# A four-layer sequence kernel on one core: router, tile sum and attention in 32-column tiles, one input share for all gates, one activation over candidate and i

## The chip, the cores and the metric

One program runs on one core of a Trainium2 chip. The metric is the device time of one execution in microseconds (us), from a handful of runs; the profiled execution gives a trace of every instruction beside its own time. A smaller time is better.

## What is computed

The input x is 2 sequences (B = 2) of 1024 tokens with 256 features, with one conditioning vector per sequence. Four layers are added to x one after the other:

```
x = x + attention(x, cond)       # 16 heads, two keys per token: a fixed one and one from cond
x = x + experts(x, cond)         # shared SwiGLU unit + top 2 of 8 GELU experts, a router picks them
x = x + (gelu(cond@W_proj+b)@W_u + x@W_e)
x = x + lstm(x, h0=cond)         # below
```

The last layer is a recurrence over the 1024 tokens and cannot be made parallel in time:

```
xz = x@Wx + b                                # (2, 1024, 4*256)
z = xz_t + prev_h @ Wh
ai, af, ao, ag = split(z, 4)                 # i, f, o and the candidate c (ag)
next_c = sigmoid(af) * prev_c + sigmoid(ai) * tanh(ag)
next_h = sigmoid(ao) * tanh(next_c)
```

All sigmoids are written as tanh of half the argument, so that one table of ScalarE serves.

## The kernel before

**Batches and steps.** The tokens are worked in 128 batches of U = 8 steps. A step is one token of both sequences. Each engine has its own program with its own loop over the batches; inside it the eight steps u = 0 to 7 are written out. Nothing but semaphores orders the engines against one another. The engines are TensorE (PE), VectorE (DVE), ScalarE (ACT), GpSimd (POOL) and SyncE (SP), which only moves x in and y out.

**The chain of one step.** PE multiplies the last h (`h_ring`) with Wh. For the gates f and i the small h is the stationary operand and the weights move (`recur_row`, 64 columns wide); the result lies in rows and DVE has to transpose it (`t_f`, `t_i`). For the candidate c and for o the weights are stationary and h moves (`recur_column`, 2 columns wide); that result needs no transpose. All of them are written in 32-column tiles: four matmuls (j = 0 to 3) that use the four column groups of the array. Each fp32 matmul of the program is two matmul instructions in the trace. Then ACT takes tanh of f, of c and of i; DVE makes `keep_out` (f times the old cell) and, by a scan, the new cell; ACT takes tanh of o and of the cell; DVE makes h, which increments `hid`, and PE's next step waits for `hid`.

**Side work.** Everything else is done for later batches between the steps: after its recurrence matmuls PE does, in u = 0, `stream_mm` and `down_mm(0)`; in u = 1 `scores` and `route`; in u = 2 `down_mm(1)` and `down_mm(2)`; in u = 3 `sum_mm` and `attend`; in u = 4 and 5 `up_mm`; in u = 6 and 7 the input share x@Wx of the next eight steps.

**The input share.** z_f, z_i, z_c and z_o hold the eight steps of a batch in PSUM. Before the change DVE copies the bias into them (`bias_f`, `bias_i`, `bias_x`) and PE adds x@Wx: `inject_x` (c and o, 128 columns wide, u = 6) and two calls of `inject` (f, i, 64 wide, u = 7). c and o come out in rows in `z_x`, and DVE transposes them at the head of the loop, in u = 0, into z_c and z_o (L689, L690); PE's first c matmul of the batch waits for that (`x_turned`).

**Names of lines.** L921 is `recur_row`, L931 `recur_column`, L709 and L711 the transposes of f and i, L507, L510, L513, L516, L519 the tanh of f, c, i, o and cell, L717 `keep_out`, L720 the scan, L738 h, L604, L607, L610 the bias copies, L767 `scores`, L777 and L779 `route`, L807 `sum_mm`, L771 `attend`, L784 `up_mm`, L790 `stream_mm` and `down_mm`, L825 and L818 the input share.

## Time and profile before

| | |
|---|---|
| time, median of 3 runs | 2076.67 us (2074.86 to 2077.8) |
| profiled execution | 2075.86 us, of which 2074.1 us are the span of the trace |
| PE matmul busy | 2023.7 us, 98% |
| PE weight loads busy | 1620.8 us, 78% |
| DVE busy | 1368.1 us, 66% |
| ACT busy | 910.0 us, 44% |
| POOL busy | 1139.5 us, 55% |
| DMA | 7 GB/s on average |

Busy is the time in which at least one instruction of the engine was under way, as a share of the span. Matmuls are pipelined and overlap one another, so 98% doesn't mean that the array has no room. The span is nearly all loop: the recurrence begins some 45 us into it and runs 128 batches.

### The profile page before, as it was taken

Reading aid. Unit: us, or ns where it says so; the run is one execution under the profiler, and the core shown is the slowest. Engines: PE = TensorE matmul, PEld = TensorE weight load, DVE = VectorE, ACT = ScalarE, POOL = GpSimd, SP = SyncE. Lnnn points to the kernel's source line nnn. Section 1 sums busy time; section 2 is a strip of 40 time slices with the busy share of each in tenths; the row PEclk is TensorE's granted clock in tenths of the full one; section 3 lists DMA queues with packets and bytes.
Section 4 is the critical chain, followed back from the end, with each engine's and each line's share of the span. In section 5 each row is a group of like instructions: output and inputs, shape, how many; then the busy total and the mean of one; then the engine's idle time right before and its main releaser. Section 6 shows DMA issues by size and latency. Waiting matters only on the chain. (4 is left out here: it accounts for less than half of the span.)

```text
span 2074.1 us, 254185 instructions
## 1 busy us (share of the span) xinstructions
PE 2023.7 (98%) x112624; PEld 1620.8 (78%) x112624; DVE 1368.1 (66%) x7216; ACT 910.0 (44%) x5781; POOL 1139.5 (55%) x4950
## 2 busy tenths in 40 slices
PE   7999999999999999999999999999999999999999
PEld 6777777777777777777777777777777777777777
DVE  2566666666666666666666666666666666666666
ACT  1344444444444444444444444444444444444444
POOL 3555555555555555555555555555555555555555
PEclk9999999999999999999999999999999999999999
DMA  4000000000000000000000000000000000000000
GB/s 160 4 3 3 3 4 3 3 3 3 3 3 4 3 3 3 3 3 3 3 3 3 3 3 3 3 3 3 3 4 3 3 3 3 3 3 4 3 3 3
DMA packets 57724, 14.67 MB, mean 7 GB/s; under 512 B 56176, under 2 KB 56304, under 8 KB 57200
## 3 DMA queue, kind: packets, MB, share of 16 engines
q1 hardware_dynamic: 57712, 14.50, 3.0%
q8 instruction: 9, 0.15, 0.0%
q14 instruction: 3, 0.02, 0.0%
HBM read 12.37 MB, written 2.10 MB: 7 GB/s over the span
## 5 line engine op out<-in xcount | busy, mean ns | idle before, releaser
L931 PE MATMUL bank<-h_ring,wh_sb 128*32 128x2 f32 x65536 | 765.6, 173 | 1.8 <-issue 1.8
L921 PEld LDWEIGHTS bank<-wh_sb,h_ring 128*2 128x2 f32 (+1 forms) x32768 | 480.0, 90 | 331.1 <-DVE h_ring L738 320.8
L931 PEld LDWEIGHTS bank<-h_ring,wh_sb 128*32 128x32 f32 x65536 | 731.0, 109 | 2.0 <-issue 2.0
L921 PE MATMUL bank<-wh_sb,h_ring 128*2 128x64 f32 (+1 forms) x32768 | 658.3, 220 | 18.0 <-issue 2.5
L507 ACT ACTIVATE f_act<-bank 128x4 f32<-128x4 f32 x1024 | 177.3, 173 | 781.3 <-DVE bank L709 772.7
L709 DVE STREAM_TRANSPOSE bank<-bank 128x64 f32<-128x64 f32 x1024 | 270.3, 264 | 312.3 <-PE bank L921 296.7
L784 PE MATMUL bank<-up_sb,x 128*32 128x512 f32 x2064 | 283.2, 606 | 0.0
L711 DVE STREAM_TRANSPOSE bank<-bank 128x64 f32<-128x64 f32 x1024 | 270.8, 264 | 0.6 <-PE bank L921 0.6
L790 PE MATMUL bank<-down_e,hid_t 128*16 128x256 f32 x3096 | 268.5, 381 | 0.6 <-ACT down_e L488 0.6
L720 DVE TENSOR_TENSOR_SCAN bank<-addend,bank 128x16 f32<-128x16 f32 x1024 | 200.3, 196 | 103.4 <-ACT bank L513 2.7
L738 DVE SCALAR_TENSOR_TENSOR h_ring<-o_act,bank 128x4 f32<-128x4 f32 x1024 | 159.9, 156 | 119.0 <-ACT bank L519 87.0
L380 POOL TENSOR_TENSOR num<-one,fall 128x8 f32<-128x8 f32 x128 | 25.6, 200 | 353.5 <-ACT fall L467 353.5
L516 ACT ACTIVATE o_act<-bank 128x4 f32<-128x4 f32 x1024 | 177.3, 173 | 70.3 <-PE bank L931 1.4
L717 DVE SCALAR_TENSOR_TENSOR addend<-f_act,bank 128x4 f32<-128x4 f32 x1024 | 165.9, 162 | 21.4
L510 ACT ACTIVATE bank<-bank 128x4 f32<-128x4 f32 x1024 | 161.8, 158 | 41.4 <-PE bank L931 2.7
L519 ACT ACTIVATE bank<-bank 128x4 f32<-128x4 f32 x1024 | 161.8, 158 | 21.4
L513 ACT ACTIVATE bank<-bank 128x4 f32<-128x4 f32 x1024 | 158.7, 155 | 0.0
L790 PEld LDWEIGHTS bank<-down_e,hid_t 128*16 128x16 f32 x3096 | 102.4, 95 | 41.3 <-issue 1.5
L386 POOL TENSOR_TENSOR num<-num 128x8 f32<-128x8 f32 x520 | 103.6, 199 | 40.8
L818 PE MATMUL bank<-wx_sb,x 128*16 128x64 f32 x4128 | 107.4, 222 | 8.7
L825 PE MATMUL bank<-wx_sb,x 128*16 128x128 f32 x2064 | 81.3, 275 | 10.0 <-issue 0.4
L432 POOL TENSOR_TENSOR hid_e<-gelu_act,gate_w 128x256 f32<-128x256 f32 x130 | 79.7, 613 | 17.2
(144 smaller groups left out, 2543.9 us busy)
## 6 DMA issues: line engine op xcount, KB each, us to landing
x_a<-in_x SPq DMA_DIRECT2D x129, 16.0 KB, 1.7
x_s<-in_x SPq DMA_DIRECT2D x129, 16.0 KB, 1.6
up_sb<-in_up SPq DMA_DIRECT2D x1, 2048.0 KB, 12.6
out_y<-y_sb SPq DMA_DIRECT2D x128, 16.0 KB, 1.4
down_sb<-in_down SPq DMA_DIRECT2D x1, 1536.0 KB, 8.1
wx_sb<-in_wx SPq DMA_DIRECT2D x1, 1024.0 KB, 14.8
wh_sb<-in_wh SPq DMA_DIRECT2D x1, 1024.0 KB, 16.8
wkv_sb<-in_wkv SPq DMA_DIRECT2D x1, 512.0 KB, 3.8
```

What stands on the lines that cost most here:

```text
L507: nc.scalar.activation(f_act[:, :].rearrange("p (c b) -> p c b", b=B), by_row(t_f)[:, :, step], ACT.Tanh).then_inc(a_f, 1)
L510: nc.scalar.activation(factor_q[:, :, 2].rearrange("p (c b) -> p c b", b=B), by_row(z_c)[:, :, step], ACT.Tanh)
L516: nc.scalar.activation(o_act[:, :].rearrange("p (c b) -> p c b", b=B), by_row(z_o)[:, :, step], ACT.Tanh)
L519: nc.scalar.activation(c_tanh, cell_c, ACT.Tanh).then_inc(cell_tanh, 1)
L709: nc.vector.transpose(t_f, z_f).then_inc(f_turned, 1)
L711: nc.vector.transpose(t_i, z_i).then_inc(i_turned, 1)
L717: nc.vector.scalar_tensor_tensor(out=keep_out, in0=f_act[:, :], scalar=1.0, in1=cell_c, op0=ALU.add, op1=ALU.mult).then_inc(terms_in, 1)
L720: nc.vector.tensor_tensor_scan(cell_all, addend[:, :], factor, 0.0, ALU.add, ALU.mult).then_inc(cell, 1)
L784: last = nc.tensor.matmul(units[32 * j:32 * (j + 1), :], src[:, c, 0, :], up_sb[:, c, j, :], start=(c == 0), stop=(c == C - 1), skip_group ...
L790: return nc.tensor.matmul(partial_b[32 * j:32 * j + NB, :], lhs, rhs, start=first, stop=False, skip_group_check=True)
L921: last = nc.tensor.matmul(z[32 * j:32 * j + row + B, :], h_ring[:, prev, c, WIN - B - row:WIN], wh_v[:, c, g, j, :], start=False, stop=(c ...
L931: last = nc.tensor.matmul(by_row(z)[32 * j:32 * (j + 1), m, row:row + B], wh_v[:, c, g, j, 32 * m:32 * (m + 1)], h_ring[:, prev, c, WIN - ...
```

## The change

1. `route`, `sum_mm` and `attend` no longer use 128-column stationary operands. Each matmul is split into four of 32 columns (j = 0 to 3), each to its own quarter of the partitions. The matmul with `pick` in `route` (L779 before) stays at 128 columns.
2. The input share of all four gates is made by one `inject` in u = 6, 256 columns wide, into a wider `z_x`; the wait for `terms_in` ahead of it is gone, and so are both injects in u = 7. DVE writes all four biases with one copy in u = 5 (`bias_x`, 256 wide in place of 128), and no longer in u = 7.
3. z_f gets its share by a copy from z_x in u = 7 (`base_f`, where `bias_f` was, with one more wait, for `x_injected`); z_i by a copy at the head of the loop in u = 0, ahead of the two transposes. PE waits for `f_based` and `i_based` in u = 0.
4. One activation makes tanh of c and of i together (8 elements a partition instead of twice 4). It waits for the count `i_and_c_in`, which DVE's transpose of i and PE's c matmuls both raise. For it t_i and z_c are placed in neighbouring banks; z_o gets a bank of its own.
5. In the part ahead of the loop the folded weights rotate through five banks instead of four, and some small results lie in other banks.

```diff
@@ -179,21 +179,28 @@
         addend = sb("addend", [P, 4 * NCELL])
         keep_out = addend[:, :].rearrange("p (q k) -> p q k", k=4)[:, :, 3]
 
-        bank = [ctx.enter_context(nc.psum_tensor(f"bank{n}", [P, 512], F32)) for n in range(8)]
-
-
-
-        z_f, z_i = bank[0][:, 0:HC], bank[1][:, 0:HC]
+        BANK = 512
+        psum = ctx.enter_context(nc.psum_tensor("psum", [P, 8 * BANK], F32))
+        bank = [psum[:, n * BANK:(n + 1) * BANK] for n in range(8)]
+
+
+
+        z_f, z_i = bank[0][:, 0:HC], bank[3][:, 0:HC]
         t_f = bank[6][:, 4 * HC:5 * HC]
-        t_i = bank[1][:, HC:2 * HC]
-        z_x = bank[2][:, HC:3 * HC]
-        z_c, z_o = bank[2][:, 0:HC], bank[3][:, 0:HC]
+        z_x = bank[2][:, 0:4 * HC].rearrange("p (g m) -> p g m", g=4)
+        z_o = bank[1][:, 0:HC]
+
+        T_I, Z_C = 3 * BANK + HC, 4 * BANK
+        t_i, z_c = psum[:, T_I:T_I + HC], psum[:, Z_C:Z_C + HC]
+        i_and_c = psum[:, T_I:T_I + 2 * (Z_C - T_I)].rearrange("p (g k) -> p g k", g=2)[:, :, 0:HC]
+        i_and_c = i_and_c.rearrange("p g (c r) -> p g c r", r=32)
...
         factor = bank[4][:, HC:HC + 4 * NCELL]
         factor_q = factor.rearrange("p (q k) -> p q k", k=4)
+        i_and_c_out = factor_q[:, :, 1:3].rearrange("p q g -> p g q")
...
-                    act.wait_ge(c_made, now)
-                    nc.scalar.activation(factor_q[:, :, 2].rearrange("p (c b) -> p c b", b=B),
-                                         by_row(z_c)[:, :, step], ACT.Tanh)
-                    act.wait_ge(i_turned, now)
-                    nc.scalar.activation(factor_q[:, :, 1].rearrange("p (c b) -> p c b", b=B),
-                                         by_row(t_i)[:, :, step], ACT.Tanh).then_inc(terms_in, 1)
+                    act.wait_ge(i_and_c_in, act.snap(t * 2 + (2 * u + 2)))
+                    nc.scalar.activation(i_and_c_out.rearrange("p g (c b) -> p g c b", b=B),
+                                         i_and_c[:, :, :, step], ACT.Tanh).then_inc(terms_in, 1)
...
-
-            def bias_f(up_to):
-                nc.vector.tensor_copy(z_f, bias_sb[:, GF, :]).then_inc(f_bias, up_to)
-
-            def bias_i(up_to):
-                nc.vector.tensor_copy(z_i, bias_sb[:, GI, :]).then_inc(i_bias, up_to)
-
             def bias_x(up_to):
-                nc.vector.tensor_copy(z_x.rearrange("p (g m) -> p g m", g=2),
-                                      bias_sb[:, GO:GC + 1, :]).then_inc(x_bias, up_to)
+
+                nc.vector.tensor_copy(z_x, bias_sb[:, :, :]).then_inc(x_bias, up_to)
+
+
+            def base_f(up_to):
+                nc.vector.tensor_copy(z_f, z_x[:, GF, :]).then_inc(f_based, up_to)
 
...
             with dve.Fori(READY, READY + T, U) as t:
@@ -685,9 +687,9 @@
                     now = dve.snap(t + (u + 1))
                     if u == 0:
 
-                        dve.wait_ge(x_injected, now)
-                        nc.vector.transpose(z_c, z_x[:, HC:2 * HC])
-                        nc.vector.transpose(z_o, z_x[:, 0:HC]).then_inc(x_turned, U)
+                        nc.vector.tensor_copy(z_i, z_x[:, GI, :]).then_inc(i_based, U)
+                        nc.vector.transpose(z_c, z_x[:, GC, :])
+                        nc.vector.transpose(z_o, z_x[:, GO, :]).then_inc(x_turned, U)
                     elif u == 1:
                         dve.wait_ge(x_ready, now)
                         dve.wait_ge(stream_made, now)
@@ -708,10 +710,11 @@
                     dve.wait_ge(f_made, now)
                     nc.vector.transpose(t_f, z_f).then_inc(f_turned, 1)
                     dve.wait_ge(i_made, now)
-                    nc.vector.transpose(t_i, z_i).then_inc(i_turned, 1)
+                    nc.vector.transpose(t_i, z_i).then_inc(i_and_c_in, 1)
                     if u == 7:
                         dve.wait_ge(f_turned, now)
-                        bias_f(U)
+                        dve.wait_ge(x_injected, now)
+                        base_f(U)
 
                     dve.wait_ge(a_f, now)
                     nc.vector.scalar_tensor_tensor(out=keep_out, in0=f_act[:, :], scalar=1.0, in1=cell_c,
@@ -728,7 +731,6 @@
                     elif u == 6:
...
-                        bias_i(U)
...
             def attend(attn, weights):
                 for c in range(C):
-                    last = nc.tensor.matmul(attn[:, c], value_w[:, c * P:(c + 1) * P], weights,
-                                            start=True, stop=True)
+                    for j in range(J):
+                        last = nc.tensor.matmul(attn[32 * j:32 * (j + 1), c],
+                                                value_w[:, c * P + 32 * j:c * P + 32 * (j + 1)], weights,
+                                                start=True, stop=True, skip_group_check=True)
                 return last
 
             def route(out, src):
                 for c in range(C):
-                    nc.tensor.matmul(out, src[:, c, :, :].rearrange("p j n -> p (j n)"), router[:, c, :],
-                                     start=(c == 0), stop=False, skip_group_check=True)
+                    for j in range(J):
+                        nc.tensor.matmul(out[32 * j:32 * (j + 1), :], src[:, c, j, :], router[:, c, :],
+                                         start=(c == 0), stop=False, skip_group_check=True)
                 nc.tensor.matmul(out, pick, route_t[:, :], start=False, stop=True,
                                  skip_group_check=True).then_inc(route_made, U)
 
@@ -804,27 +809,21 @@
 
             def sum_mm():
                 for c in range(C):
-                    last = nc.tensor.matmul(x3_b[:, c, :], partial[:, c * P:(c + 1) * P], sum_tiles,
-                                            start=True, stop=True)
+                    for j in range(J):
+                        last = nc.tensor.matmul(x3_b[32 * j:32 * (j + 1), c, :],
+                                                partial[:, c * P + 32 * j:c * P + 32 * (j + 1)], sum_tiles,
+                                                start=True, stop=True, skip_group_check=True)
                 return last
...
-            def inject(z, g):
+            def inject():
 
                 for c in range(C):
                     for j in range(J):
-                        last = nc.tensor.matmul(z[32 * j:32 * j + NB, :], x3[:, c, NB:2 * NB], wx_v[:, c, g, j, :],
-                                                start=False, stop=False, skip_group_check=True)
-                return last
-
-            def inject_x():
-                for c in range(C):
-                    for j in range(J):
-                        last = nc.tensor.matmul(z_x[32 * j:32 * j + NB, :].rearrange("p (g m) -> p g m", g=2),
-                                                x3[:, c, NB:2 * NB], wx_v[:, c, GO:GC + 1, j, :],
-                                                start=False, stop=False, skip_group_check=True)
+                        last = nc.tensor.matmul(z_x[32 * j:32 * j + NB, :, :], x3[:, c, NB:2 * NB], wx_v[:, c, :, j, :],
+                                                start=False, stop=(c == C - 1), skip_group_check=True)
                 return last
...
                     prev = (u - 1) % U
                     now = pe.snap(t + (u + 1))
                     pe.wait_ge(hid, now)
+                    if u == 0:
+                        pe.wait_ge(f_based, now)
                     recur_row(z_f, GF, u * B, prev).then_inc(f_made, 1)
+                    if u == 0:
+                        pe.wait_ge(i_based, now)
                     recur_row(z_i, GI, u * B, prev).then_inc(i_made, 1)
                     if u == 0:
                         pe.wait_ge(x_turned, now)
-                    recur_column(z_c, GC, u * B, prev).then_inc(c_made, 1)
+                    recur_column(z_c, GC, u * B, prev).then_inc(i_and_c_in, 1)
                     recur_column(z_o, GO, u * B, prev).then_inc(o_made, 1)
...
                     elif u == 6:
-
-                        pe.wait_ge(terms_in, pe.snap(t * 2 + (2 * u + 2)))
                         pe.wait_ge(x_bias, now)
-                        inject_x().then_inc(x_injected, U)
-                    elif u == 7:
-                        pe.wait_ge(f_bias, now)
-                        inject(z_f, GF)
-                        pe.wait_ge(i_bias, now)
-                        inject(z_i, GI)
+                        inject().then_inc(x_injected, U)
```

The first place is DVE's row at the head of the loop, u = 0. Before:

```order
L683 ISA
L689 STREAM_TRANSPOSE bank<-bank 128x64 [waits x_injected]
L690 STREAM_TRANSPOSE bank<-bank 128x64
L709 STREAM_TRANSPOSE bank<-bank 128x64 [waits f_made]
L711 STREAM_TRANSPOSE bank<-bank 128x64 [waits i_made]
```

And of the changed kernel:

```order
L690 COPY psum<-psum 128x64
L691 STREAM_TRANSPOSE psum<-psum 128x64
L692 STREAM_TRANSPOSE psum<-psum 128x64
L710 REGISTER_ALU
L711 STREAM_TRANSPOSE psum<-psum 128x64 [waits f_made]
L713 STREAM_TRANSPOSE psum<-psum 128x64 [waits i_made]
```

The copy of z_i now stands ahead of the two transposes; the wait and the register instruction for it (ISA) are gone from the head.

The second place is PE's row from the c and o matmuls of u = 6 to the end of the loop. Before:

```order
L931 MATMUL bank<-h_ring,wh_sb 32x2 x32
L976 ISA
L825 MATMUL bank<-wx_sb,x 16x128 [waits x_bias,terms_in]
L825 MATMUL bank<-wx_sb,x 16x128 x7
L941 REGISTER_ALU
L921 MATMUL bank<-wh_sb,h_ring 16x64 [waits hid]
L921 MATMUL bank<-wh_sb,h_ring 16x64 x15
L931 MATMUL bank<-h_ring,wh_sb 32x2 x32
L818 MATMUL bank<-wx_sb,x 16x64 [waits f_bias]
L818 MATMUL bank<-wx_sb,x 16x64 x7
L818 MATMUL bank<-wx_sb,x 16x64 [waits i_bias]
L818 MATMUL bank<-wx_sb,x 16x64 x7
```

And of the changed kernel:

```order
L926 MATMUL psum<-h_ring,wh_sb 32x2 x32
L825 MATMUL psum<-wx_sb,x 16x256 [waits x_bias]
L825 MATMUL psum<-wx_sb,x 16x256 x7
L936 REGISTER_ALU
L916 MATMUL psum<-wh_sb,h_ring 16x64 [waits hid]
L916 MATMUL psum<-wh_sb,h_ring 16x64 x15
L926 MATMUL psum<-h_ring,wh_sb 32x2 x32
L932 REGISTER_ALU
L932 COMPARE_AND_BRANCH
```

All of the input share now stands in u = 6, and in u = 7 the loop's branch comes right behind the recurrence matmuls.

The third place is ACT's row in a step. Before:

```order
L507 ACTIVATE f_act<-bank 128x4 [waits f_turned]
L510 ACTIVATE bank<-bank 128x4 [waits c_made]
L513 ACTIVATE bank<-bank 128x4 [waits i_turned]
L516 ACTIVATE o_act<-bank 128x4 [waits o_made]
L519 ACTIVATE bank<-bank 128x4 [waits cell]
```

And of the changed kernel:

```order
L517 ACTIVATE f_act<-psum 128x4 [waits f_turned]
L519 REGISTER_ALU
L520 ACTIVATE psum<-psum 128x2x4 [waits i_and_c_in]
L523 ACTIVATE o_act<-psum 128x4 [waits o_made]
L526 ACTIVATE psum<-psum 128x4 [waits cell]
```

Two activations became one, with a register instruction ahead of it that works out the count to wait for.

## Rows read from the trace of the kernel before

**Rows 1.** Page, busy time of each engine, share of the span, instructions.

```profile
PE 2023.7 (98%) x112624; PEld 1620.8 (78%) x112624; DVE 1368.1 (66%) x7216; ACT 910.0 (44%) x5781; POOL 1139.5 (55%) x4950
```

**Rows 2.** Timeline (start us, us, engine, line, x instructions), PE L921: first matmuls of steps.

```profile
1000.19 0.63 PE L921 MATMUL bank<-wh_sb,h_ring 128*4 128x64 f32 x32
...
1002.22 0.63 PE L921 MATMUL bank<-wh_sb,h_ring 128*6 128x64 f32 x32
...
1004.12 0.64 PE L921 MATMUL bank<-wh_sb,h_ring 128*8 128x64 f32 x32
...
1006.24 0.64 PE L921 MATMUL bank<-wh_sb,h_ring 128*10 128x64 f32 x32
...
1008.14 0.66 PE L921 MATMUL bank<-wh_sb,h_ring 128*12 128x64 f32 x32
...
1010.03 0.66 PE L921 MATMUL bank<-wh_sb,h_ring 128*14 128x64 f32 x32
...
1011.92 0.64 PE L921 MATMUL bank<-wh_sb,h_ring 128*16 128x64 f32 x32
...
1014.08 0.63 PE L921 MATMUL bank<-wh_sb,h_ring 128*2 128x64 f32 x32
...
1015.97 0.63 PE L921 MATMUL bank<-wh_sb,h_ring 128*4 128x64 f32 x32
```

**Rows 3.** Timeline, step u = 5 of the same batch.

```profile
1008.59 0.73 PE L931 MATMUL bank<-h_ring,wh_sb 128*32 128x2 f32 x63
...
1008.84 0.27 DVE L711 STREAM_TRANSPOSE bank<-bank 128x64 f32<-128x64 f32 x1
...
1008.91 0.17 ACT L507 ACTIVATE f_act<-bank 128x4 f32<-128x4 f32 x1 [1.03 <-DVE bank L709]
...
1009.13 0.16 ACT L510 ACTIVATE bank<-bank 128x4 f32<-128x4 f32 x1
1009.15 0.19 PEld L784 LDWEIGHTS bank<-up_sb,x 128*32 128x32 f32 x8
...
1009.20 0.15 ACT L513 ACTIVATE bank<-bank 128x4 f32<-128x4 f32 x1
1009.39 0.20 DVE L720 TENSOR_TENSOR_SCAN bank<-addend,bank 128x16 f32<-128x16 f32 x1
...
1009.49 0.27 DVE L610 COPY bank<-bias_sb 128x128 f32<-128x128 f32 x1
...
1009.81 0.16 DVE L738 SCALAR_TENSOR_TENSOR h_ring<-o_act,bank 128x4 f32<-128x4 f32 x1
```

**Rows 4.** Groups by line and form, ACT, from 80 to 2070 us.

```profile
L467 ACT ACTIVATE fall<-bank 128x8 f32<-128x8 f32 x126 | 22.3, 177 | 71.1 <-PE bank L779 71.1
```

**Rows 5.** Timeline, side work of u = 3.

```profile
1005.25 0.62 PE L807 MATMUL bank<-small_sb,partial 128*128 128x16 f32 x4
```

**Rows 6.** Timeline, side work and h of u = 1.

```profile
1001.25 0.27 PE L767 MATMUL bank<-x_s,score_w 128*32 128x16 f32 x4
...
1001.86 0.16 DVE L738 SCALAR_TENSOR_TENSOR h_ring<-o_act,bank 128x4 f32<-128x4 f32 x1
```

**Rows 7.** Timeline, side work of u = 2.

```profile
1003.25 1.07 PE L790 MATMUL bank<-down_e,hid_t 128*16 128x256 f32 x16
```

**Rows 8.** Timeline, DVE across the end of the loop, u = 7 to u = 0.

```profile
1013.28 0.20 DVE L607 COPY bank<-bias_sb 128x64 f32<-128x64 f32 x1
...
1013.62 0.14 DVE L738 SCALAR_TENSOR_TENSOR h_ring<-o_act,bank 128x4 f32<-128x4 f32 x1
...
1013.97 0.27 DVE L689 STREAM_TRANSPOSE bank<-bank 128x64 f32<-128x64 f32 x1 [0.22 <-issue]
...
1014.15 0.22 DVE L690 STREAM_TRANSPOSE bank<-bank 128x64 f32<-128x64 f32 x1
```

**Rows 9.** Windows: busy of PE, PEld, DVE, ACT, POOL; clock; DMA share; GB/s.

```profile
56.20:63.00 6.80, 6.21 (x203) 3.89 (x196) 2.14 (x12) 1.28 (x10) 4.49 (x19) 0.50 0.03 6
...
1000.00:1008.00 8.00, 8.00 (x431) 6.72 (x426) 5.29 (x28) 3.61 (x23) 3.08 (x13) 1.00 0.04 6
```

More of the change, by code:

```diff
@@ L39 @@
 BLOCKS = UNITS * KS
-FOLD = (0, 1, 2, 3)
+FOLD = (0, 1, 2, 3, 4)
 FOLD_1, FOLD_2 = 3, 7
@@ L209, in cond_stack_kernel @@
         attn_first_b = bank[6][:, 128:128 + 2 * C * NB].rearrange("p (c n t) -> p c n t", c=C, n=2)
+        route_t_b = bank[7][0:B, 448:448 + E]
+        u_b = bank[6][:, 400:400 + C * B].rearrange("p (c b) -> p c b", b=B)
+        cond_b = bank[6][:, 408:408 + C * B].rearrange("p (c b) -> p c b", b=B)
         route_first_b = bank[5][:, 64:64 + 2 * E].rearrange("p (n e) -> p n e", n=2)
@@ L270, in cond_stack_kernel @@
         x3_out = sem("x3_out")
-        z_ready = sem("z_ready")
         moved = sem("moved")
         bias_scaled = sem("bias_scaled")
-        f_bias = sem("f_bias")
-        i_bias = sem("i_bias")
         x_bias = sem("x_bias")
+        f_based = sem("f_based")
+        i_based = sem("i_based")
         x_injected = sem("x_injected")
@@ L281, in cond_stack_kernel @@
         i_made = sem("i_made")
-        c_made = sem("c_made")
         o_made = sem("o_made")
         f_turned = sem("f_turned")
-        i_turned = sem("i_turned")
+        i_and_c_in = sem("i_and_c_in")
         a_f = sem("a_f")
@@ L341, in _ @@
             pool.sem_inc(y_stored, 16)
-            for s in (f_made, i_made, c_made, o_made, f_turned, i_turned, a_f, cell, cell_tanh, hid, x_turned):
+            for s in (f_made, i_made, o_made, f_turned, a_f, cell, cell_tanh, hid, x_turned, i_based):
                 pool.sem_inc(s, READY)
             pool.sem_inc(terms_in, 2 * READY)
+            pool.sem_inc(i_and_c_in, 2 * READY)
             pool.sem_inc(own_out, READY)
@@ L443, in _ @@
             weigh(2 * U).then_inc(hid_e_out, 2 * U)
-            pool.wait_ge(z_ready, 1)
+            pool.wait_ge(x_injected, READY)
             move().then_inc(moved, READY + U)
@@ L627, in _ @@
             dve.wait_ge(value_made, 2)
-            nc.vector.tensor_copy(route_t[0:B, :], bank[4][0:B, 0:E]).then_inc(value_out, 1)
+            nc.vector.tensor_copy(route_t[0:B, :], route_t_b).then_inc(value_out, 1)
             dve.wait_ge(w_in["x_first"], 16)
@@ L639, in _ @@
             dve.wait_ge(u_made, 1)
[L640 to L641 removed]
+            nc.vector.tensor_tensor(u_in[:, :, :], u_b, pairs(b_proj2), ALU.add).then_inc(u_in_out, 1)
             dve.wait_ge(w_in["bias_z"], 16)
@@ L650, in _ @@
             dve.wait_ge(cond_made, 1)
-            nc.vector.tensor_copy(cond_t[:, :, :], bank[4][:, D:D + C * B].rearrange("p (c b) -> p c b", b=B)
-                                  ).then_inc(cond_done, 1)
+            nc.vector.tensor_copy(cond_t[:, :, :], cond_b).then_inc(cond_done, 1)
             dve.wait_ge(hid_e_out, U)
@@ L663, in _ @@
             invert_s(2 * U)
+            hidden_a(2 * U)
+            hidden_s(2 * U)
+            dve.wait_ge(fold_out, BLOCKS)
             dve.wait_ge(terms_set, 1)
@@ L680, in _ @@
             invert_inv(2 * U)
+            dve.wait_ge(x_injected, READY)
+            base_f(READY + U)
             dve.wait_ge(terms_set, 3)
@@ L839, in _ @@
             for c in range(C):
-                last = nc.tensor.matmul(bank[4][0:B, 0:E], cond[:, c, :], router_t[:, c, :],
+                last = nc.tensor.matmul(route_t_b, cond[:, c, :], router_t[:, c, :],
                                         start=(c == 0), stop=(c == C - 1))
@@ L879, in _ @@
                 for c in range(C):
-                    last = nc.tensor.matmul(bank[4][:, 64 + m * B:64 + (m + 1) * B],
+                    last = nc.tensor.matmul(u_b[:, m, :],
                                             wproj2_sb[:, c, m * P:(m + 1) * P],
@@ L893, in _ @@
                 for m in range(C):
-                    last = nc.tensor.matmul(bank[4][:, D + c * B:D + (c + 1) * B], wu_sb[:, m, c * P:(c + 1) * P],
+                    last = nc.tensor.matmul(cond_b[:, c, :], wu_sb[:, m, c * P:(c + 1) * P],
                                             u_act[:, m, :], start=(m == 0), stop=(m == C - 1))
@@ L908, in _ @@
             pe.wait_ge(x_bias, READY)
-            inject_x().then_inc(x_injected, READY + U)
-            pe.wait_ge(f_bias, READY)
-            inject(z_f, GF)
-            pe.wait_ge(i_bias, READY)
-            inject(z_i, GI).then_inc(z_ready, 1)
+            inject().then_inc(x_injected, READY)
             pe.wait_ge(own_first, 2)
@@ L974, in _ @@
                     elif u == 6:
-                        pe.wait_ge(terms_in, pe.snap(t * 2 + (2 * u + 2)))
                         pe.wait_ge(x_bias, now)
-                        inject_x().then_inc(x_injected, U)
-                    elif u == 7:
-                        pe.wait_ge(f_bias, now)
-                        inject(z_f, GF)
-                        pe.wait_ge(i_bias, now)
-                        inject(z_i, GI)
+                        inject().then_inc(x_injected, U)
 _INS = ("x", "small", "wkv", "wq", "wproj", "up", "we", "down", "wproj2", "wu", "wx", "wh", "bias_z")
```

7 lines of the change are left out of this document (removed).

## The prediction

> **What bounds the kernel now.** I read the page first. PE is busy 98% of the span, the others 66% or less [rows 1]. That says only that some matmul is nearly always under way, so I went to the timeline of one batch. The starts of the first matmul of each step [rows 2] give the lengths: u = 1 takes 2.03 us (1000.19 to 1002.22), u = 2 1.90, u = 3 2.12, u = 4 1.90, u = 5 1.89, u = 6 1.89, u = 7 2.16, u = 0 1.89; together 15.78 us. 128 batches make 2020 of the 2074 us span. Three steps stand out: u = 1 by 0.14 us, u = 3 by 0.23, u = 7 by 0.27 over 1.89.
>
> What sets 1.89 is seen in u = 5 [rows 3], which begins at 1008.14 [rows 2]. The c and o matmuls begin 0.45 us later (1008.59). ACT's tanh of c starts at 1009.13, that of i at 1009.20, 0.07 behind it and not earlier, though i was transposed by 1009.11. It ends at 1009.35, the scan starts at 1009.39, h at 1009.81, that is 1.67 after the step's start, ends at 1009.97, and 0.06 later PE begins the next step. This is the h chain.
>
> There is a second limit of nearly the same length, the array itself. In u = 2 the 16 side matmuls of 256 columns begin at 1003.25 [rows 7] and the next step at 1004.12, 0.87 later; in u = 5 the weights of `up_mm` begin to load at 1009.15 [rows 3] and the next step starts at 1010.03, 0.88 later. 0.45 for f and i, 0.56 for c and o (1008.59 to 1009.15) and 0.87 make 1.88 to 1.90: a step with this much side work can't be shorter, however early h is. That holds for u = 2, 4 and 5, and, as an estimate, for u = 0: its 12 matmuls of 256 columns give two of the column groups four each, as in u = 2.
>
> **Tiles in u = 3.** `sum_mm` is four instructions from 1005.25 on [rows 5], `attend` four more, and the next step begins 0.99 after 1005.25: 0.12 for each. The h chain would have allowed 1004.12 + 1.67 + 0.16 + 0.06 = 1006.01; it was 1006.24. Now there are 32 instructions of 32 columns, spread over the four column groups. The nearest row is L931, the same tile form with a 2-column moving operand: 63 in 0.73, less 0.17 for the last, so 0.009 apart [rows 3]. 32 of them take 0.29. They may begin at 1005.13 (two thirds of the 0.12 before were a change of form, my estimate) and are over long before 1006.0. u = 3 falls back to the h chain: 0.23 gained. Cover gone, it would be lost again only if the tiles took over 0.8 us.
>
> **Tiles in u = 1.** h ends at 1002.02 [rows 6] and the next step could start at 1002.08; it starts at 1002.22. The router's four instructions of 128 columns (0.12 each, as in u = 3, 0.47 in all) become 16 of 0.009, 0.15 in all. `pick` stays. The array is free at 1002.22 - 0.32 = 1001.90, before h. Gained: 0.14.
>
> **One activation.** It starts when the later of c and i is ready: c at 1009.13 as L510 did, i at 1009.11 plus some 0.03. It lasts 0.16, as L510; four more elements cost under 0.01 (L467 with 8 columns lasts 177 ns [rows 4], L507 with 4 columns 0.17 [rows 3]). So it ends at 1009.30 instead of 1009.35, and the scan comes 0.05 earlier. `keep_out` is done by then. ACT's new register instruction falls in the 0.22 between L507 and L510. This 0.05 counts only in steps that the h chain sets: all of it in u = 3, some 0.02 in u = 1 (there the transposes come later, behind `attended`), and in u = 7. In u = 0, 2, 4, 5 the array takes it back.
>
> **u = 6.** The inject is now 16 instructions of 256 columns, the form of [rows 7]; it need not wait for `terms_in`. It becomes a step at the array's limit: 1.89 to 1.90 instead of 1.89. Lost: 0.01. The bias copy in u = 5 grows from 128 to 256 columns. 64 columns take 0.20 [rows 8], 128 take 0.27 [rows 3], so 256 some 0.40: from 1009.44 to 1009.84. h may start up to 0.05 late by it, which the array's limit hides.
>
> **The loop's end.** PE starts u = 0 at 1014.08, 0.32 after h ended (1013.62 + 0.14 [rows 8]) instead of 0.06: its last inject and its branch lie there. Both are out of the way now. But DVE has a chain of its own: its first instruction of the batch starts 0.35 after h starts (1013.97), the second 0.18 later, ends at 1014.37, and PE needs it for c at 1014.08 + 0.45 = 1014.53. Now h starts at 1.67 - 0.05 = 1.62 of the step, at 1013.54 (the copy of bias i that stood between is gone). Behind it come the copy of z_i, the two transposes, and 0.05 or 0.06 to PE. Slow ends: 1013.54 + 0.35 + 0.18 + 0.18 + 0.22 + 0.06 = 1014.53, nothing gained. Fast ends: the order shows the register instruction gone from the head, so 0.28 instead of 0.35 (an estimate), and a 0.20 long operation lets the next start 0.10 later (L720 to L610 [rows 3]): 1014.38, 0.15 gained. z_i reaches PE in time in both: copied by 1014.15 at the latest, its matmuls done 0.22 later. I take 0.09, nearer to the fast end because of the shorter copy. It is passed on whole: after c, u = 0 runs at the array's limit.
>
> **The sum.** u = 3 0.23 + 0.05, u = 1 0.14 + 0.02, loop's end 0.09, u = 6 -0.01: 0.52 us a batch, 66.6 us in 128. Ahead of the loop 48 narrow injects become 16 wide ones and some matmuls are tiled; some tenths to 2 us, I take 2. The profiled execution took 2075.86, so 2007 us. The median of the runs is 0.8 above it, within their spread of 3 us.
>
> **Rival 1: the small tiles are not side by side.** `scores` has four instructions of 32 columns in one column group, 0.27 less 0.17, so 0.03 apart [rows 6]. If 8 or 16 moving columns cost that much on all groups, u = 3 has 32 x 0.03 = 0.96 of side work, from 1005.13 to 1006.09 and a next step at 1006.15: 0.09 gained. u = 1 has 0.48, as before: nothing. With 0.09 at the loop's end and -0.01: 0.17, 22 us, 2054 us. For it: the narrow form is not shown with these operands. Against: L931 is narrower still and runs at 0.009. The Trainium skill has a rule in this direction (TensorEngine Tiling (Array Packing), Performance Considerations, Instruction Overhead): each matmul has about 60 cycles of overhead, and one should not tile a dimension where the moving side is already small. By it, at 25 ns each, the 32 instructions would take 0.80, the 16 router ones 0.40, the sum 0.38 a batch and the time some 2027 us; L931's rows go against its use here.
>
> **Rival 2: only the tiles gain.** The activation of both waits for the slower of two and its wider form costs what it saves; the loop's end goes by its slow values. Then 0.23 + 0.14 - 0.01 = 0.36, 46 us, 2030 us.
>
> **Rival 3, slower: the clock.** From 56.2 to 63.0 us the granted clock was 0.50 (the 1.2 GHz level), and 203 matmuls were done in 6.8 us; at 1.00 it was 431 in 8.0, which is 366 in 6.8 [rows 9]. Such a stretch loses 3.0 us. The change leaves PE idle for some 0.7 us in u = 7, 0.5 in u = 3 and 0.1 to 0.2 in u = 1, where it was working. If the clock falls for that, it decides from 23 such stretches on (69 / 3.0); one in every batch makes 2007 + 128 x 3.0 = 2391 us. Against: the columns that move through the array in a batch stay the same, some only pass from u = 7 to u = 6, and no stretch of the loop's steady part was below 1.00.
>
> **How the numbers follow.** Forecast 0.77 (own range 1994 to 2020), rival 2 0.12, rival 1 0.05, rival 3 0.05, else 0.01. The low end is 0.30 + 0.19 + 0.15 = 0.64 a batch, 1994; the high end 0.23 + 0.12 - 0.03 = 0.32, 2035. I give 1992 to 2034. This kernel's measurement tells 0.2%, 4 us, from no change. All cases but the clock are faster by more: faster 0.93, same 0.01, slower 0.06.
>
> **What the profile after would show.** L916 starts: u = 3 at 1.84, u = 1 at 1.87, u = 7 and 0 together some 3.96 instead of 4.05, the rest unchanged, a batch 15.26. L813 and L774 together under 0.5 us. The merged activation 0.16 long, the scan 0.05 behind its end or less, 1.20 after the step's start. At the loop's head c is released by `x_turned`, not by the f and i matmuls. The forecast is wrong if u = 2, 4 or 5 get shorter (the array is not the limit there), if u = 0's c starts over 0.1 later than I say, or if PEclk falls in the loop.

## The result and the profile after

2004.42 us, median of 4 runs (2002.88 to 2006.19), against 2075.93 (2074.86 to 2077.8): ratio 0.9655, 95% interval 0.9638 to 0.9672. The forecast was 2007 in 1992 to 2034. The profiled execution took 2006.19 us, its span 2004.4. Ratios here and below compare the means of a kernel's runs without those over 1.5% above its fastest, which leaves runs out only for pad16 and route_tiles.

The page of the kernel after: busy time of each engine, share of the span, instructions; the granted clock in tenths over 40 slices; the queue that brings instructions (packets, MB); then groups of instructions (busy, mean ns, idle before and its releaser).

```profile
PE 1848.3 (92%) x113164; PEld 1462.6 (73%) x113164; DVE 1351.8 (67%) x7215; ACT 812.2 (41%) x4757; POOL 1134.2 (57%) x4950
...
PEclk9899999999999999999999999999999999999999
...
q8 instruction: 9, 0.15, 0.0%
...
L916 PEld LDWEIGHTS psum<-wh_sb,h_ring 128*2 128x2 f32 (+1 forms) x32768 | 519.6, 90 | 446.0 <-DVE h_ring L740 414.9
...
L723 DVE TENSOR_TENSOR_SCAN psum<-addend,psum 128x16 f32<-128x16 f32 x1024 | 199.2, 195 | 71.4 <-ACT psum L520 29.3
...
L520 ACT ACTIVATE psum<-psum 128x8 f32<-128x8 f32 x1024 | 165.9, 162 | 73.6 <-DVE psum L713 31.7
```

PE is busy 92% instead of 98% [rows 1], or 175 us less. Of these, 70 us shortened the span and 106 us became idle time, most of it waits for h: ahead of the weight loads of the row matmuls they are 415 us (L740) where the page before has 321. The clock stays up. The activation over i and c takes 162 ns for 8 columns. The clock and the instruction queue seem to say nothing here; an experiment makes both matter.

The timeline of a batch, first matmul of each step from u = 0 to the next u = 0 (they answer to [rows 2], which begin at u = 1):

```profile
1010.97 0.84 PE L916 MATMUL psum<-wh_sb,h_ring 128*2 128x64 f32 x32 [0.63 <-DVE h_ring L740]
...
1013.04 0.67 PE L916 MATMUL psum<-wh_sb,h_ring 128*4 128x64 f32 x31
...
1014.96 0.63 PE L916 MATMUL psum<-wh_sb,h_ring 128*6 128x64 f32 x32
...
1016.87 0.64 PE L916 MATMUL psum<-wh_sb,h_ring 128*8 128x64 f32 x32
...
1018.69 0.64 PE L916 MATMUL psum<-wh_sb,h_ring 128*10 128x64 f32 x32 [0.33 <-DVE h_ring L740]
1020.59 0.66 PE L916 MATMUL psum<-wh_sb,h_ring 128*12 128x64 f32 x32
...
1022.48 0.66 PE L916 MATMUL psum<-wh_sb,h_ring 128*14 128x64 f32 x32
...
1024.37 0.66 PE L916 MATMUL psum<-wh_sb,h_ring 128*16 128x64 f32 x32
...
1026.20 0.41 PE L916 MATMUL psum<-wh_sb,h_ring 128*2 128x64 f32 x16 [0.63 <-DVE h_ring L740]
```

u = 3 now takes 1.82 (1016.87 to 1018.69), u = 1 1.92, u = 0 2.07, u = 7 1.83. Single steps differ by 0.01 to 0.02, so I compare medians over all batches but the first five. Worked out from those same starts, in us:

```
               u0     u1     u2     u3     u4     u5     u6     u7    batch
before        1.882  2.032  1.904  2.118  1.899  1.895  1.882  2.153  15.77
after         2.076  1.919  1.904  1.823  1.899  1.894  1.886  1.824  15.23
two_acts      2.130  1.882  1.903  1.881  1.898  1.893  1.884  1.887  15.36
wide_sum_att. 2.076  1.920  1.903  2.117  1.898  1.893  1.884  1.826  15.52
only_merge    1.834  2.080  1.904  2.118  1.899  1.895  1.824  2.097  15.65
stream_u7     2.064  1.825  1.904  1.825  1.900  1.894  1.885  1.825  15.12
wide_route    2.079  2.086  1.904  1.825  1.900  1.894  1.886  1.825  15.40
zi_u7         1.950  1.917  1.904  1.825  1.899  1.894  1.885  1.826  15.10
both_u7       1.937  1.825  1.904  1.825  1.900  1.894  1.885  1.825  15.00
up_split      1.934  1.823  1.904  1.989  1.825  1.832  1.894  1.825  15.03
```

Gained per batch: u = 3 0.295, u = 7 and u = 0 together 0.135, u = 1 0.113, u = 6 -0.004: 0.54, 69 us of the 71.5.

The side work of u = 3 on PE, and ACT and DVE in the same step (timeline, some rows of each):

```profile
1017.88 0.20 PE L813 MATMUL psum<-small_sb,partial 128*32 128x16 f32 x1
1017.90 0.30 PE L813 MATMUL psum<-small_sb,partial 128*32 128x16 f32 x13
...
1018.06 0.30 PE L774 MATMUL psum<-w_own,value_w 128*32 128x16 f32 x14
...
1017.64 0.17 ACT L517 ACTIVATE f_act<-psum 128x4 f32<-128x4 f32 x1
1017.86 0.16 ACT L520 ACTIVATE psum<-psum 128x8 f32<-128x8 f32 x1
...
1018.06 0.19 DVE L723 TENSOR_TENSOR_SCAN psum<-addend,psum 128x16 f32<-128x16 f32 x1
```

32 small tiles lie between 1017.88 and 1018.36; before, 8 wide ones took from 1005.25 to the next step at 1006.24 [rows 5]. The activation ends at 1018.02 and the scan starts 0.04 behind it, 1.19 after the step's start; before, in u = 5, it was 1009.39 - 1008.14 = 1.25 [rows 2, 3].

### The profile page after: what moved, and what is told of

Read it like the earlier page. It is cut to its first block and busy times, and to the rows that moved or that the text cites. A ratio compares the mean times of both kernels' runs of the same rounds, so it can differ in the third digit from the quotient of the medians.

```text
span 2004.4 us, 255266 instructions
## 1 busy us (share of the span) xinstructions
PE 1848.3 (92%) x113164; PEld 1462.6 (73%) x113164; DVE 1351.8 (67%) x7215; ACT 812.2 (41%) x4757; POOL 1134.2 (57%) x4950
## 5 line engine op out<-in xcount | busy, mean ns | idle before, releaser
L916 PEld LDWEIGHTS psum<-wh_sb,h_ring 128*2 128x2 f32 (+1 forms) x32768 | 519.6, 90 | 446.0 <-DVE h_ring L740 414.9
L916 PE MATMUL psum<-wh_sb,h_ring 128*2 128x64 f32 (+1 forms) x32768 | 690.8, 219 | 138.7 <-DVE h_ring L740 121.4
L926 PE MATMUL psum<-h_ring,wh_sb 128*32 128x2 f32 x65536 | 768.7, 173 | 3.5 <-issue 3.5
L926 PEld LDWEIGHTS psum<-h_ring,wh_sb 128*32 128x32 f32 x65536 | 725.0, 109 | 13.3 <-issue 3.7
L517 ACT ACTIVATE f_act<-psum 128x4 f32<-128x4 f32 x1024 | 177.2, 173 | 763.7 <-DVE psum L711 755.1
L711 DVE STREAM_TRANSPOSE psum<-psum 128x64 f32<-128x64 f32 x1024 | 264.6, 258 | 306.6 <-PE psum L916 306.4
L789 PE MATMUL psum<-up_sb,x 128*32 128x512 f32 x2064 | 282.7, 605 | 0.0
L713 DVE STREAM_TRANSPOSE psum<-psum 128x64 f32<-128x64 f32 x1024 | 270.6, 264 | 16.1 <-PE psum L916 3.0
L795 PE MATMUL psum<-down_e,hid_t 128*16 128x256 f32 x3096 | 268.0, 381 | 0.6 <-ACT down_e L498 0.6
L723 DVE TENSOR_TENSOR_SCAN psum<-addend,psum 128x16 f32<-128x16 f32 x1024 | 199.2, 195 | 71.4 <-ACT psum L520 29.3
L740 DVE SCALAR_TENSOR_TENSOR h_ring<-o_act,psum 128x4 f32<-128x4 f32 x1024 | 163.0, 159 | 116.8 <-ACT psum L526 87.7
L523 ACT ACTIVATE o_act<-psum 128x4 f32<-128x4 f32 x1024 | 177.4, 173 | 129.6 <-PE psum L926 2.5
```

The lines of the kernel that those rows point to most:

```text
L517: nc.scalar.activation(f_act[:, :].rearrange("p (c b) -> p c b", b=B), by_row(t_f)[:, :, step], ACT.Tanh).then_inc(a_f, 1)
L523: nc.scalar.activation(o_act[:, :].rearrange("p (c b) -> p c b", b=B), by_row(z_o)[:, :, step], ACT.Tanh)
L711: nc.vector.transpose(t_f, z_f).then_inc(f_turned, 1)
L713: nc.vector.transpose(t_i, z_i).then_inc(i_and_c_in, 1)
L723: nc.vector.tensor_tensor_scan(cell_all, addend[:, :], factor, 0.0, ALU.add, ALU.mult).then_inc(cell, 1)
L740: nc.vector.scalar_tensor_tensor(out=h_ring[:, u, :, WIN - B:WIN], in0=o_act[:, :].rearrange("p (c b) -> p c b", b=B), scalar=1.0, in1=c_t ...
```

## The experiments

All times are medians; ratios are to the kernel before, on the same chip, with 95% intervals. `+` and `-` are against the kernel after, where not said otherwise.

**two_acts.** The changed kernel with the two activations apart.

```diff
-  act.wait_ge(i_and_c_in, ...);  activation(i_and_c_out, i_and_c[:, :, :, step])
+  act.wait_ge(c_made, now);      activation(factor_q[:, :, 2], z_c[step])
+  act.wait_ge(i_turned, now);    activation(factor_q[:, :, 1], t_i[step])
```

> The changed kernel with the merged activation undone: tanh of c and of i are two instructions again, each with its own wait. Theory (the h chain and the array limit take turns): the 0.05 us an activation saves counts only where the h chain sets the step, in u = 3 and u = 7 (0.055 each) and in u = 0, whose c now starts late (0.05, up to the array's limit); in u = 1 the scan waits for keep_out, in u = 2, 4, 5, 6 for the array. So 0.16 us a batch more, 20 us, about 2025 us. Rival A (it counts in every step): 8 x 0.055 = 0.44 a batch, 2060 us. Rival B (merging is worth nothing, since the wide one waits for the slower of two): 2004 us.

2023.09 us (0.9747, 0.9733 to 0.9760). u = 3 and u = 7 lose 0.058 and 0.063 (table), as a gap of 0.05 to 0.07 between the two activations [rows 3] would have it. u = 2, 4, 5 don't move. But u = 0 loses 0.054 and u = 1 gains 0.037. The merge is worth 0.135 a batch in the kernel after, 17 us in 128 batches; the medians differ by 18.7.

**wide_sum_attend.** `sum_mm` and `attend` as `for c: matmul(out[:, c], w[:, c * P:(c + 1) * P], ...)`, 128 columns each.

> The changed kernel with sum_mm and attend at 128 columns again (route stays in tiles). Theory: u = 3 goes from 1.82 back to 2.12 us, the other steps stay, 0.295 x 128 = 38 us, 2042 us. Rival (the gain of u = 3 is partly the earlier h by the merged activation, and the wide matmuls cost less than 0.12 each once the h chain is shorter): u = 3 at about 2.06, 2034 us.

2047.15 us (0.9862, 0.9847 to 0.9877). u = 3 is back at 2.117. Of the 42.7 us this is 0.294 x 128 = 38. Most of the rest lies ahead of the loop, whose first step comes 45.6 us after the span's start instead of 42.2.

**only_merge.** The kernel before with the merged activation and its adjacent banks, nothing else.

> The kernel before with nothing but the merged activation (t_i and z_c in neighbouring banks). Theory: in that kernel the side matmuls set u = 1, 2, 3, 4 and 5 and tie in u = 0; only u = 6 is set by the h chain (-0.055), and in u = 7 the second bias copy, and with it the last inject, comes 0.05 earlier. So -0.06 to -0.11 a batch, 2062 to 2069 us: a part that is worth 20 us in the changed kernel is worth a half or less here. Rival (worth the same everywhere): -20 us, 2056 us; counted in all steps -56 us, 2020 us.

2062.46 us (0.9934, 0.9920 to 0.9947). u = 6, 7 and 0 gain 0.058, 0.056 and 0.048; u = 1 loses 0.048; u = 3, held by its side work, gains nothing. The losing u = 1 was not in the expectation.

**wide_route.** The router in 128 columns again.

> The changed kernel with the router's matmuls at 128 columns again (sum_mm and attend stay in tiles). Theory: four instructions of 0.12 in place of 16 of 0.009, 0.32 us more side work; it would end at 2.08 of the step, u = 1 goes from 1.92 to 2.08, 0.16 x 128 = 20 us, 2025 us. Rival (u = 1 is set by attended alone, the router hides behind it): 2004 us.

2030.00 us (0.9773, 0.9757 to 0.9788), 5 us over the expectation. u = 1 loses 0.167; the first step comes 2.4 us later than in the kernel after.

**stream_u7.** In the kernel after, the wait of u = 1 is on VectorE: `attended` (L588) waits for `stream_made`, which TensorE gives after the down matmuls of u = 0. Its timeline on DVE:

```profile
1012.82 0.16 DVE L740 SCALAR_TENSOR_TENSOR h_ring<-o_act,psum 128x4 f32<-128x4 f32 x1 [0.23 <-ACT psum L526]
1013.43 0.29 DVE L588 TENSOR_TENSOR x<-psum,x_a 128x128 f32<-128x128 f32 x1 [0.46 <-PE psum L795]
1013.64 0.26 DVE L711 STREAM_TRANSPOSE psum<-psum 128x64 f32<-128x64 f32 x1
1013.80 0.26 DVE L713 STREAM_TRANSPOSE psum<-psum 128x64 f32<-128x64 f32 x1
1014.13 0.16 DVE L720 SCALAR_TENSOR_TENSOR addend<-f_act,psum 128x4 f32<-128x4 f32 x1
1014.33 0.20 DVE L723 TENSOR_TENSOR_SCAN psum<-addend,psum 128x16 f32<-128x16 f32 x1
```

The step began at 1013.04; `attended` starts 0.39 into it, the f transpose (L711) behind it at 0.60, where in u = 3 it starts 0.47 in. The edit moves `stream_mm` from u = 0 to u = 7 (and once ahead of the loop, for the first batch):

```diff
   elif u == 0: pe.wait_ge(hid_st, now)
-      stream_mm(x1)
       down_mm(0).then_inc(stream_made, U)
+  elif u == 7: stream_mm(x1)
```

> The changed kernel with stream_mm moved from u = 0 to u = 7 of the batch before, where PE is idle for 0.7 us; u = 0 keeps down_mm(0). The attended x1 of u = 1 waits for the end of this side work. Theory: u = 1 is longer than forecast (1.92 instead of 1.87) because attended starts late behind stream_made and pushes both transposes; with 0.43 us less side work ahead it starts right behind h, u = 1 falls to 1.83 and u = 0 by 0.01: -0.10 a batch, 13 us, 1991 us. Rival (u = 1 is late for the double wait in front of attended or for the tiled route): the step stays at 1.92, 2002 to 2004 us.

1992.46 us (0.9595, 0.9582 to 0.9609): u = 1 falls by 0.094 to the h chain's 1.825.

**only_tiles.** The kernel before with the 32-column tiles in route, sum and attend, nothing else.

> The kernel before with nothing but the tiles in route, sum_mm and attend. Theory: u = 1 falls from 2.03 to 1.88, u = 3 from 2.12 to 1.89, no other step changes: -0.38 x 128 = -49 us, 2027 us. Rival (each small matmul has its own overhead of some 0.03): u = 3 falls by 0.09 only, 2064 us.

**3088.06 us** (1.4878, 1.4853 to 1.4903), a thousand over the expected 2027. The page of this kernel, the lines that answer to those of after:

```profile
PE 2371.9 (77%) x117292; PEld 1825.7 (59%) x117292; DVE 1351.9 (44%) x7216; ACT 876.1 (28%) x5781; POOL 1136.6 (37%) x4950
...
PEclk8787887878778888788778887887878878777878
...
q8 instruction: 577, 9.45, 1.5%
...
L926 PEld LDWEIGHTS bank<-wh_sb,h_ring 128*2 128x2 f32 (+1 forms) x32768 | 661.0, 102 | 766.1 <-issue 470.4
...
L936 PE MATMUL bank<-h_ring,wh_sb 128*32 128x2 f32 x65536 | 920.8, 180 | 214.8 <-issue 213.1
```

Three lines are new. The instruction queue moved 577 packets of 16 KB instead of 9; 470 us of the waits ahead of L926's weight loads have the releaser "issue", that is, nothing the profile shows; and the clock is at 7 and 8 tenths throughout. The theory from here: TensorE's loop no longer fits in what it keeps of its program. In one batch there are 878 matmuls (as the trace counts them) before, 882 after, 914 here, and each is two instructions, a weight load and a multiply. The Trainium skill (Runtime: NRT & Kernel Launch, Instruction fetch mechanics) gives the place: TensorE holds 2048 instructions, filled in 16 KiB blocks of 256, and a taken branch whose target isn't in the current window of two blocks stalls until it is fetched. The same section calls the cost of merely crossing a block "mostly hidden". The stall behind the branch is what the traces below show; the window is not two blocks there.

**zi_u7 and both_u7.** zi_u7 takes the copy of z_i out of the loop's head:

```diff
   if u == 0:
-      tensor_copy(z_i, z_x[:, GI, :]).then_inc(i_based, U)
       transpose(z_c, ...)
   elif u == 7:
+      base_i(U)      # the same copy, behind the scan; once ahead of the loop too
```

both_u7 is zi_u7 and stream_u7 together.

> The changed kernel with the copy of z_i moved from the head of the loop (u = 0) to u = 7, behind the scan. Theory: at the head DVE's three instructions in a row release c 0.28 us after PE could begin it; with two of them x_turned comes 0.14 earlier, while h of u = 7 is 0.02 later: -0.10 to -0.12 a batch, 13 to 15 us, about 1990 us. Rival (the head's time is the branch and the fetch behind it, which any first instruction pays, and the transposes wait for it anyway): 2002 to 2004 us.

> stream_mm and the copy of z_i both moved to u = 7. Theory: the two gains add, since one shortens u = 1 and the other u = 0: -0.20 to -0.22 a batch, 26 to 28 us, about 1977 us. Rival (with c earlier in u = 0 the array's limit of u = 0 or attended takes the gain back): 1988 us or more.

1989.05 us (0.9575, 0.9561 to 0.9588): u = 0 falls by 0.126. Together 1976.65 us (0.9513, 0.9500 to 0.9527), the fastest kernel here; the two gains, 12.0 and 15.4, add up to 27.4 of the 27.8 measured.

**pad32, pad16, route_tiles.** Three tests of the code length. The pads add one or two calls of `attend` in u = 7 of the kernel after, where PE is idle; route_tiles is the kernel before with only the router tiled.

> The changed kernel with two more calls of attend on TensorE in step u = 7 of each batch: 32 more matmuls of 64 columns, which write the values that are there already. The trace of the changed kernel leaves TensorE idle for over 0.4 us there, and 16 such matmuls took some 0.15 us, so by their time alone they are hidden. Theory A, the length of TensorE's loop is what made only_tiles slow (914 hardware matmuls per batch against 882 in the changed kernel): this kernel has 914 again, so it goes to 2700 to 3200 us, with some hundred packets on the instruction queue instead of 9 and a granted clock of about 0.8. Theory B, it was something else in only_tiles (the small tiles among the wide input copies, the clock by itself, its buffers): 2000 to 2010 us with 9 packets.

> The changed kernel with one more call of attend in step u = 7: 898 hardware matmuls per batch, halfway between the 882 that ran well and the 914 that did not. Theory A puts the limit somewhere between the two: either 2000 to 2010 us with 9 packets on the instruction queue, or some hundred packets and 2300 us or more. Theory B: 2000 to 2010 us.

> The kernel before with the router alone in 32-column tiles: 890 hardware matmuls per batch. If its loop still fits, theory A says that it keeps what the tiles are worth: step u = 1 loses 0.10 to 0.17 us (wide_route lost 0.167 there the other way), so 2054 to 2064 us, 9 packets on the instruction queue. If small tiles cost something on their own in the kernel before (theory B), 2080 us or more.

3032.45 us (1.4584, 1.4547 to 1.4622) with 577 instruction packets, 2891.67 (1.3858, 1.3775 to 1.3941) with 496, and 2361.45 (1.1257, 1.1176 to 1.1338) with 171. Matmuls that write again what is there already, placed in idle time, cost 1028 and 887 us over the kernel after. So the tiles of sum, attend and route are not the cause by themselves, and the matmuls' own time is not either. I had expected route_tiles to fit and take 2054 to 2064 us, and it shows best what happens, since most of its batches are undisturbed. Windows of one run of batches (columns as in [rows 9]):

```profile
1194.30:1209.90 15.60, 15.23 (x899) 12.10 (x894) 10.59 (x58) 7.05 (x45) 8.75 (x38) 1.00 0.02 3
...
1225.70:1256.80 31.10, 22.20 (x898) 16.99 (x890) 10.91 (x58) 6.61 (x45) 10.12 (x43) 0.73 0.04 6
1256.80:1274.00 17.20, 16.51 (x886) 12.94 (x890) 10.17 (x54) 6.97 (x45) 7.29 (x33) 0.90 0.02 3
1274.00:1289.60 15.60, 15.25 (x902) 12.12 (x897) 10.60 (x57) 7.05 (x45) 8.75 (x38) 1.00 0.02 3
```

The same, within the long batch, and the timeline at its head:

```profile
1225.70:1230.60 4.90, 0.11 (x8) 0.00 (x0) 0.40 (x2) 0.00 (x0) 1.35 (x5) 0.94 0.07 10
1230.60:1238.00 7.40, 7.33 (x272) 5.99 (x276) 2.86 (x14) 1.77 (x13) 0.36 (x2) 0.50 0.04 7
1238.00:1247.00 9.00, 7.17 (x290) 5.54 (x284) 3.34 (x18) 2.21 (x15) 4.31 (x18) 0.69 0.04 7
```

```profile
1230.67 1.03 PE L922 MATMUL bank<-wh_sb,h_ring 128*2 128x64 f32 x32 [4.86 <-issue]
...
1241.61 0.62 PE L932 MATMUL bank<-h_ring,wh_sb 128*32 128x2 f32 x53 [0.57 <-issue]
...
1245.48 0.54 PE L932 MATMUL bank<-h_ring,wh_sb 128*32 128x2 f32 x27 [1.26 <-issue]
```

The branch back ends a batch, and PE does nothing for 4.86 us. Then the clock is at the 1.2 GHz level (0.50). Windows cut finer show it there from 1230.0 to 1240.2, again from 1243.7 to 1250.5, and in the next batch from 1257.4 to 1260.7, with 1.00 between. Shorter stalls follow the first; whether they fall where a block ends is not shown. Of the 15.5 us that the batch loses, 8.5 are more idle time of PE (31.10 - 22.20 against 0.37). In the other 7.0 PE is busy longer with the same matmuls, in a batch whose mean clock is 0.73. From the branches' times, of the 127 batches behind the first 18 are this long (30.6 us in the mean), 19 take 17.5, 90 take 15.6; 162 packets more than before are 9 for each of the 18, the loop once over. Pad16 has 54 such batches and 487 packets more, pad32 63 and 568: 9 each again.

In an undisturbed batch of route_tiles the next starts are 1323.12 and 1325.00, so u = 1 takes 1.88 instead of 2.03 [rows 2]:

```profile
1323.12 0.63 PE L922 MATMUL bank<-wh_sb,h_ring 128*4 128x64 f32 x32
1325.00 0.63 PE L922 MATMUL bank<-wh_sb,h_ring 128*6 128x64 f32 x32
```

That is the router's tiles alone, 0.15 a batch, which the reloads bury under some 300 us (18 x 15.0 + 19 x 1.9).

**up_split.** both_u7 with `up_mm` cut by columns and a loop kept short:

```diff
+def up_mm(c, src, cols): ... matmul(units[32 * j:32 * (j + 1), cols], src[:, c, 0, :], up_sb[:, c, j, cols], ...)
 u == 3:  sum_mm();  attend(...)           # attend in 2 tiles of 64 columns instead of 4 of 32
+         up_mm(0, x1, 0:96);  up_mm(1, x1, 0:96)
-u == 4:  up_mm(0, x1)
+u == 4:  up_mm(0, x1, 96:512)
-u == 5:  up_mm(1, x1)
+u == 5:  up_mm(1, x1, 96:512)
-u == 1:  pe.wait_ge(x_ready, now)
```

> The kernel of both_u7 with the hidden units' matmuls (up_mm) cut in two ranges of columns: columns 0 to 96 of both c in step u = 3 behind attend, the other 416 in u = 4 and u = 5, which held all 512 each. To keep TensorE's loop short, attend goes in two tiles of 64 columns in place of four of 32, and TensorE's own wait for x_ready in u = 1 is dropped (VectorE waits for it before it makes x1, for which TensorE waits). In one batch there are 890 hardware matmuls and 11 or 12 other TensorE instructions, 1791 or 1792 in all; both_u7 has 1776, route_tiles, which was reloaded in about one batch in five, 1793. Theory A1, the loop runs undisturbed up to 1792 instructions (7 pieces of 256, which is what one 16 KB packet of the instruction queue would hold at 64 bytes each): 9 packets, and what the cut is worth shows: the wait of u = 4 and u = 5 behind their own side matmuls (1.899 and 1.894 us steps, where those with less beside them take 1.825) goes, 2 x 0.07 x 128 = 18 us, so 1956 to 1963 us. Theory A2, the limit lies lower: some hundred packets and 2100 us or more, with undisturbed batches of 14.85 us between. If the steps u = 4 and u = 5 are held by something other than their side matmuls: 1976 us, and if u = 3 grows too long with its 0.16 us of new matmuls: 1965 us or more.

1980.86 us (0.9543, 0.9527 to 0.9559), instruction queue 9 packets: the loop fits, but the time is 4 us above both_u7, not the expected 1956 to 1963. With the sequencer's own records (8 register operations, 1 branch, 1 register pair, 1 separate wait) it has 2 x 890 + 11 = 1791 instructions in a batch and runs undisturbed; route_tiles has 2 x 890 + 13 = 1793 and doesn't. 1792 is 7 blocks of 256. The Trainium skill's 2048 instructions (the same section) are 8 blocks; that one of them must be free for the block that comes next would give 7, but this is my inference, not shown. Either way a loop far longer than two blocks runs undisturbed. The length of TensorE's whole program does not tell the kernels apart as well: with what the trace shows outside the loop, up_split has 2320 instructions, both_u7, which is undisturbed, 2337, and route_tiles 2338.

u = 4 and u = 5 fall to 1.825 and 1.832: they were held by their side matmuls. u = 3 grew by 0.164, which is where the expected gain went. Its side work in the timeline of up_split:

```profile
1004.27 0.33 PE L817 MATMUL psum<-small_sb,partial 128*32 128x16 f32 x15
1004.53 0.41 PE L778 MATMUL psum<-w_own,value_w 128*64 128x16 f32 x8
1004.87 0.54 PE L793 MATMUL psum<-up_sb,x 128*32 128x96 f32 x16
1005.23 0.29 PE L921 MATMUL psum<-wh_sb,h_ring 128*10 128x64 f32 x7
```

Eight instructions of 64 columns take from 1004.53 to 1004.87, 0.043 each; sixteen of 32 columns took 0.13 to 0.15. The new part of `up_mm` takes another 0.36, up to 1005.23, where I had expected 0.16. Both are over what I had counted on, and no run separates them.

## Why the prediction was right, point by point

- **u = 3**: 0.23 + 0.05 forecast, 0.295 measured. With wide tiles all of it is lost (wide_sum_attend, 0.294), with two activations 0.058 of it (two_acts): the tiles bring the step back to the h chain, the merge shortens the chain. The tiles begin 1.01 into the step, as forecast, and their spacing, 0.009 taken from L931, is (0.30 - 0.18) / 13 = 0.009. Rival 1 falls: its 0.03 was the spacing within one column group [rows 6], and here each of the four groups gets an instruction every 4 x 0.009 = 0.036 in the mean. The Trainium skill (TensorEngine Tiling (Array Packing), Performance Considerations, Instruction Overhead) gives each matmul about 60 cycles of overhead, 25 ns in the prediction. By these rows the trace disagrees only if the 60 cycles are paid one after another over all groups, as the prediction applied them; paid within each group they fit both 0.036 and 0.03. The Trainium skill's advice there is against a tiling factor from a dimension that is already small; here the factor comes from the 128 stationary columns.
- **Loop's end**: 0.09 forecast, 0.135 measured, by two errors of opposite sign. DVE's chain and the first c matmul of u = 0:

```profile
1010.75 0.16 DVE L740 SCALAR_TENSOR_TENSOR h_ring<-o_act,psum 128x4 f32<-128x4 f32 x1
1011.11 0.23 DVE L690 COPY psum<-psum 128x64 f32<-128x64 f32 x1 [0.20 <-issue]
1011.25 0.26 DVE L691 STREAM_TRANSPOSE psum<-psum 128x64 f32<-128x64 f32 x1
1011.41 0.22 DVE L692 STREAM_TRANSPOSE psum<-psum 128x64 f32<-128x64 f32 x1
...
1011.69 0.70 PE L926 MATMUL psum<-h_ring,wh_sb 128*32 128x2 f32 x63
```

  From h's start to c it is 1011.69 - 1010.75 = 0.94; I took 0.90, between 0.84 and 0.99. The first gap is 0.36, as before, not the 0.28 of my fast end. But from c to the next step's start it is 1013.04 - 1011.69 = 1.35, where "after c, u = 0 runs at the array's limit" gave 0.56 + 0.87 = 1.43. The step that failed is that sentence: u = 0's twelve matmuls of 256 columns leave room, and h sets its end (1012.82 + 0.16, and PE starts 0.06 later). two_acts and only_merge agree: u = 0 moves by 0.054 and 0.048 with the merge. zi_u7 shows that the copy at the head of this chain costs 0.126.
- **u = 1**: 0.16 forecast, 0.113 measured. The step that failed is "some 0.02 in u = 1". The merge is worth -0.04 there, not +0.02 (only_merge 0.048 lost, two_acts 0.037 gained without it): when u = 0 ends sooner, the side work that u = 1's `attended` waits for does not, so u = 1 gives back what u = 0 gained. stream_u7 removes the wait and the step is at 1.825. The tiles' own part, 0.14, holds: 0.15 alone on the kernel before, 0.167 in the kernel after.
- **Which limit holds where**: u = 2, 4 and 5 did not move under any edit that touched only the h chain, as forecast, and up_split shows the array's limit in 4 and 5 by taking it away.
- **u = 6**: -0.01 forecast, -0.004 measured. only_merge shows what the old order could have had, 1.824: the wide inject gives up 0.06 there.
- **The sum**: 0.52 forecast, 0.54 measured: u = 1 0.05 too high, the loop's end 0.045 and u = 3 0.015 too low. Part of the closeness is that these offset. The first step comes 2.4 us earlier, near the 2 us forecast, but the first batch takes 1.7 us more (24.8 instead of 23.1), so that 0.7 us is left. That the tiles and injects did it is not shown: in only_merge, which leaves those matmuls alone, the first step comes 2.4 us later than before.
- **Rival 2** took the merge to be worth nothing; it is worth 17 to 19 us. **Rival 3**, the clock, did not come: the page's clock is 9 in every slice of the loop but the early one at 8. Its price was too low, though, and its cause another. I took 3.0 us for a stretch, from [rows 9]; in the batch of the 4.86 us stall some 7.0 went to the lower clock. And I looked for the cause in idle time of 0.1 to 0.7 us between matmuls; with it in every batch of the kernel after, the clock stays up. Behind the first few batches of the loop it fell only in the kernels that reload the loop. The tiles add 36 matmuls to a batch (878 to 914), and the wide inject takes 48 narrow ones down to 16 (914 to 882). So the loop of the kernel after has 2 x 882 + 12 = 1776 instructions, 15 below the longest that ran undisturbed. The prediction counted instructions for their time, never for their room, and no rival held this case; the inject's part of the change, for which I forecast -0.01 a batch, is what lets the tiles pay.

What stays open: whether the limit lies at 1792 for any place of the loop in the program, or only where it starts as here; why a loop of 1793 is reloaded in some batches and not in all; and whether up_split with attend in 32-column tiles would gain its 0.14 a batch, for which the loop has no room.
